# VectorE's side work regrouped by slot in the second mixers, with whole parameter rows in DRAM

## The reference, cut to what matters

```python
def _mamba(x, Win, convw, convb, Wx, Wdt, bdt, Alog, Dp, Wout):
    xz = x @ Win
    xi, z = jnp.split(xz, 2, axis=-1)
    xi = jax.nn.silu(_causal_dwconv(xi, convw, convb))
    xdbc = xi @ Wx
    dt_in = xdbc[..., :DT_RANK]
    Bm = xdbc[..., DT_RANK:DT_RANK + D_STATE]
    Cm = xdbc[..., DT_RANK + D_STATE:]
    dt = jax.nn.softplus(dt_in @ Wdt + bdt)
    A = -jnp.exp(Alog)
    y = _selective_scan(xi, dt, A, Bm, Cm, Dp)
    return y * jax.nn.silu(z) @ Wout
...
    yf = _mamba(x, fw_Win, fw_convw, fw_convb, fw_Wx, fw_Wdt, fw_bdt, fw_Alog, fw_D, fw_Wout)
    yf = _layernorm(yf + x, fwn_w, fwn_b)
    yb = _mamba(jnp.flip(x, 1), bw_Win, bw_convw, bw_convb, bw_Wx, bw_Wdt, bw_bdt, bw_Alog, bw_D, bw_Wout)
    yb = _layernorm(jnp.flip(yb, 1) + x, fwn_w, fwn_b)
    y = yf + yb
```

## Time and profile before

| | us |
|---|---|
| median of 3 runs | 3485.58 |
| lowest, highest | 3485.55, 3494.75 |
| the profiled execution | 3482.14 |
| its span in the profile | 3480.3 |

### The profile page before, as it was taken

The page is one execution under the profiler, slowest core; times in us unless marked ns, Lnnn a source line. Parts: engine busy times, 40 slices in busy tenths (PEclk is TensorE's granted clock), DMA queues, the critical chain, the costliest instruction groups (busy, mean ns, idle before and its releaser), DMA issues. The chain is left out here.

```text
span 3480.3 us, 25090 instructions
## 1 busy us (share of the span) xinstructions
PE 2788.0 (80%) x7782; PEld 1181.9 (34%) x7782; DVE 2847.1 (82%) x2257; ACT 1775.0 (51%) x2375; POOL 2241.3 (64%) x1102
## 2 busy tenths in 40 slices
PE   6677777666577888888888888788888787779899
PEld 2223222454223333333333333333333332234344
DVE  6999899542369999999999999999999999578300
ACT  5775776231355655555655555565555654233211
POOL 3696499001339889899889889788888898401000
PEclk7899799878879999999999999999999999889899
DMA  2011011247436656666756666665666666421000
GB/s 64 31 48 36 26 49 48 71 153 273 159 86 176 172 171 163 178 180 165 182 171 174 175 176 179 168 174 168 176 168 175 178 165 200 114 92 49 12 18 24
DMA packets 245973, 451.46 MB, mean 130 GB/s; under 512 B 22448, under 2 KB 51312, under 8 KB 245808
## 3 DMA queue, kind: packets, MB, share of 16 engines
q1 hardware_dynamic: 240080, 428.89, 43.8%
q0 software_dynamic: 5760, 20.97, 1.5%
HBM read 414.94 MB, written 34.87 MB: 129 GB/s over the span
## 5 line engine op out<-in xcount | busy, mean ns | idle before, releaser
L1394 POOL TENSOR_TENSOR mix_prod<-mix_spread,mix_h 128x1024 f32<-128x1024 f32 x512 | 1335.7, 2612 | 249.3 <-DVE mix_h L1818 118.7
L1926 PE MATMUL mix_banks<-mix_prod,kept_ident 128*128 128x512 f32 x2048 | 1035.9, 631 | 117.4 <-POOL mix_prod L1394 84.6
L1444 ACT ACTIVATE mix_side_in<-mix_dt,mix_neg_a 128x1024 f32<-128x1024 f32 x384 | 437.6, 1141 | 308.5 <-DVE mix_h L1818 305.1
L1926 PEld LDWEIGHTS mix_banks<-mix_prod,kept_ident 128*128 128x128 f32 x2048 | 396.6, 199 | 555.6 <-issue 296.5
L1804 DVE TENSOR_TENSOR mix_banks<-mix_banks,mix_dtu 128x1024 f32<-128x1024 f32 x384 | 466.6, 1215 | 9.6 <-PE mix_banks L1916 6.5
L1818 DVE TENSOR_TENSOR_SCAN mix_h<-mix_side_in,mix_state,mix_banks 128x1024 f32<-128x1024 f32 x192 | 450.6, 2347 | 17.4
L1818 DVE TENSOR_TENSOR_SCAN mix_h<-mix_side_in,mix_banks 128x1024 f32<-128x1024 f32 x192 | 439.0, 2286 | 19.2 <-ACT mix_side_in L1444 1.8
L410 POOL TENSOR_TENSOR mix_drive<-mix_drive,mix_du 128x1024 f32<-128x1024 f32 x128 | 304.8, 2399 | 150.7 <-ACT mix_drive L481 150.7
L1404 POOL TENSOR_TENSOR mix_side_in<-mix_spread,mix_dtu 128x512 f32<-128x512 f32 x256 | 340.5, 1330 | 13.4 <-issue 6.7
L1916 PE MATMUL mix_banks<-mix_parts,kept_sel 96*128 96x512 bf16 x384 | 153.9, 401 | 210.8 <-DVE mix_h L1818 203.3
L633 DVE TENSOR_TENSOR_SCAN mix_h<-mix_banks,mix_state,mix_drive 128x1024 f32<-128x1024 f32 x128 | 296.1, 2340 | 14.2 <-POOL mix_drive L410 9.3
(11 more groups left out here) (270 smaller groups left out, 4471.3 us busy)
## 6 DMA issues: line engine op xcount, KB each, us to landing
mix_spread<-par_rows SPq DMA_DIRECT2D x640, 512.0 KB, 5.9
mix_c_row<-c_rows SPq DMA_DIRECT2D x40, 512.0 KB, 3.5
exa_f<-f SPq DMA_DIRECT2D x32, 512.0 KB, 6.9
slot_outputs<-exa_inter POOLq DMA_DIRECT2D x32, 512.0 KB, 7.2
ln_zp<-slot_outputs SPq DMA_DIRECT2D x8, 2048.0 KB, 7.7
first_acc<-xT SPq DMA_DIRECT2D x8, 512.0 KB, 8.2
x_scratch<-first_acc POOLq DMA_DIRECT2D x8, 512.0 KB, 3.2
fw_scratch<-mix_res SPq DMA_DIRECT2D x8, 512.0 KB, 9.1
```

Source lines behind the costliest of these rows:

```text
L1394: pool.tensor_tensor(prod[:, un % 2, :], spread[:, i % SLOTS, :], h[:, un % HR, :], ALU.mult).then_inc(prod_ready, 1)
L1444: act.activation(drive[un % 2] if pooled(un) else side_in[:, un % 2, :], dt[:, at // NS, :], ACT.Exp, scale=neg_a[:, way(p), at:at + 1]).t ...
L1926: mm = pe.matmul(y_bank[:, hf, :], k.ident[:], half(prod[:, un % 2, :], hf), start=False, stop=True, skip_group_check=True)
```

## The change

Four things are changed, all in `mixer1`.
- Tables of VectorE's side work: `soft` of group 1 from slots (5, 6, 8) to (5, 8, 9), of group 2 from (15, 16, 19) to (16, 17, 20), of group 3 from (24, 25, 26) to (24, 25, 28). `conv` from (29, 30, 31), (35, 36, 37), (41, 42, 43) to (29, 32, 33), (36, 37, 38), (40, 41, 44). For the pass behind: `joined` of the first half from 32, 33 to 36, 37; of the second half `near_root` 29 to 30, `root_of` 41 to 40, `normed` 46, 47 to 48, 49, `joined` 48, 49 to 52, 53. `less_mid` from 55 to 56, and ScalarE's `split_low` behind it from 56 to 57. One pair of matmuls on TensorE goes from slot 37 to 38 and ScalarE's copy of it from 38 to 39.
- `par_rows` in DRAM holds one row of 1024 steps for each state, where it held two of 512. A load of a row takes one piece of 4 KB for a partition, and was two of 2 KB.
- The store of these rows is four DMAs of 16 partitions and was one of 64; SP makes it in slot 55 and not 53, and waits for it in slot 62.
- SP's other steps come later: `load_yf` in slots 32 and 42 (26 and 37), `store` in 41 and 57 (36 and 53).

```diff
-    par_rows = nc.dram_tensor("par_rows", (NP, 2, 2, NS, TT), F32, kind="Internal").ap()
+    par_rows = nc.dram_tensor("par_rows", (NP, 2, NS, TC), F32, kind="Internal").ap()
...
-                    if s == 26:
+                    if s == 32:
                         load_yf(p - 1, 0)
-                    if s == 36:
+                    if s == 41:
                         store(p - 1, 0)
...
-                if p + 1 < NP and s == 53:
+                if p + 1 < NP and s == 55:
                     sp.wait_ge(c_kept, p + 2)
-                    sp.dma_start(par_rows[p + 1].rearrange("k h n t -> (k h n) t"), rows[0:64, :]).then_inc(c_stored, 16)
-                    sp.wait_ge(c_stored, 16 * (p + 2))
+                    for kind in range(2):
+                        for hf in range(2):
+                            r0 = 32 * kind + NS * hf
+                            sp.dma_start(half(par_rows[p + 1, kind], hf), rows[r0:r0 + NS, :]).then_inc(c_stored, 16)
+                if p + 1 < NP and s == 62:
+                    sp.wait_ge(c_stored, 4 * 16 * (p + 2))
...
-                row = par_rows[un // UNITS, 1 if kind == "c" else 0, :, n:n + 1, :].rearrange("h o t -> o h t")
-                sp.dma_start(spread[:, i % SLOTS, :].rearrange("p (h t) -> p h t", h=2), row.broadcast_to((P, 2, TT))
+                row = par_rows[un // UNITS, 1 if kind == "c" else 0, n:n + 1, :]
+                sp.dma_start(spread[:, i % SLOTS, :], row.broadcast_to((P, TC))
...
-                    for hf, at in enumerate(((17, 20, 21, 22, 32, 33), (29, 41, 46, 47, 48, 49))):
+                    for hf, at in enumerate(((17, 20, 21, 22, 36, 37), (30, 40, 48, 49, 52, 53))):
...
-                    for g, at in ((1, (5, 6, 8)), (2, (15, 16, 19)), (3, (24, 25, 26))):
+                    for g, at in ((1, (5, 8, 9)), (2, (16, 17, 20)), (3, (24, 25, 28))):
```

More of the change, by code:

```diff
@@ L1145, in __init__ @@
             if p + 1 < passes:
-                for n, s in enumerate((25, 27, 32, 33, 34, 36, 37, 39)):
+                for n, s in enumerate((25, 27, 32, 33, 34, 36, 38, 39)):
                     order.append((s, 0, ("xi", p + 1, n // 2, n % 2)))
@@ L1320, in side @@
                 if p >= 1:
[L1321 removed]
+                    if s == 32:
                         load_yf(p - 1, 0)
[L1323 removed]
+                    if s == 41:
                         store(p - 1, 0)
[L1325 removed]
+                    if s == 42:
                         load_yf(p - 1, 1)
[L1327 removed]
+                    if s == 57:
                         store(p - 1, 1)
[L1329 removed]
+                if p + 1 < NP and s == 55:
                     sp.wait_ge(c_kept, p + 2)
[L1331 to L1332 removed]
+                    for kind in range(2):
[4 more added lines that the diff above has]
+                    sp.wait_ge(c_stored, 4 * 16 * (p + 2))
                 if p == WAY - 1 and s == 4:
@@ L1519, in keep_par @@
                 if p:
-                    act.wait_ge(c_stored, 16 * p)
+                    act.wait_ge(c_stored, 4 * 16 * p)
                 act.activation(rows[:], bank[0:96, :], ACT.Copy).then_inc(c_kept, 1)
@@ L1612, in side @@
                         tap_matrices(1)
-                    for n, s0 in enumerate((26, 28, 33, 34, 35, 37, 38, 40)):
+                    for n, s0 in enumerate((26, 28, 33, 34, 35, 37, 39, 40)):
                         if s == s0:
@@ L1772, in side @@
                 if ahead:
-                    for g, at in enumerate(((29, 30, 31), (35, 36, 37), (41, 42, 43))):
+                    for g, at in enumerate(((29, 32, 33), (36, 37, 38), (40, 41, 44))):
                         if s in at:
@@ L1777, in side @@
                         rest_of(p + 1)
-                    if s == 55:
+                    if s == 56:
                         less_mid(p + 1)
@@ L1947, in side @@
                 if ahead:
-                    for n, s0 in enumerate((25, 27, 32, 33, 34, 36, 37, 39)):
+                    for n, s0 in enumerate((25, 27, 32, 33, 34, 36, 38, 39)):
                         if s == s0:
```

2 lines of the change are left out of this document (removed).

## The result

| | before | after |
|---|---|---|
| median of 7 runs each, us | 3489.73 | 3500.55 |
| lowest to highest | 3485.55 to 3494.75 | 3499.22 to 3505.08 |
| the profiled execution (its span) | 3482.14 (3480.3) | 3505.08 (3503.3) |

The ratio is 1.0032, with a 95% interval of 1.0021 to 1.0044: slower by 10.8 us (7 to 15). The time is inside the range, near its upper end. The likeliest case was no change, which the prediction bounded at 0.3%; the measured 0.32% lies on that bound, and its interval reaches to both sides of it.

The account below looks back on a forecast made before the run. VectorE was taken to bound the second mixers, with about 71 us of port waiting (instruction time over its minimum, from taking turns with GpSimd) movable. Terms summed to +0.7 us, giving a forecast median of 3486 us, range 3460 to 3503.

Parts of the forecast that it names:

- (a): SP's later store of parameter rows: waits in slot 55 and nearly all left in 57 and 58 go, -12.8 us.
- (b): SP's later load of the forward result: GpSimd no longer starves, taps of slots 29 and 30 stop waiting, -5.0 us.
- (c): Whole rows in DRAM land in 4 to 5 us, not 5.9; VectorE waits less in slots 4 to 9, -8 us (0 to -15).
- (d): Moved joins (L1745): most of their 4.3 us of waiting goes, -3 us (0 to -4.3).
- (e): Slot 20: `soft` step behind `root_of` waits 2.2 us in each of 7 passes, +15.4 us (0 to 16.8).
- (f): Slots 36 and 37: a tap behind `joined` waits in passes 5 and 6, +8.8 us (0 to 9.6).
- (g): Pair of `root_of` and tap moved from slot 41 to 40 waits a whole product, +2.4 us (-11 to +4).
- (h): `soft` steps moved from slots 15, 16 to 16, 17 wait 19.8 us against 18.9, +0.9 us (-10 to +9).
- (i): The other moved side steps, some 40, start first in their slots at 0.05 us each, +2 us.
- random arrivals: Rival, chance 0.01: 11 moved steps meet GpSimd at random moments in each of 8 passes, waiting 88 us; 3574 us.
- GpSimd late in slots of kind 0 and 1: Rival, chance 0.19: side steps moved where GpSimd has product and half drive wait more; slots 8, 9, 16, 17 priced; 3502 us.
- The pairs cost nothing: Rival, chance 0.15: TensorE's add delays GpSimd's product over 0.6 us in slots 20, 36, 37, 40; both instructions pass; 3448 us.

## Why the prediction was right and wrong

The sum said +0.7 us, and 10.8 was measured; beside it, the port waiting grew by 20.6 to 25.3 us, for which VectorE's idle time gave back up to 8.4. By its steps, with the port waiting of the two profiled executions:

| step | predicted | seen |
|---|---|---|
| (a) store of rows | -12.8 | -10.0 here; -14.6 alone |
| (b) load_yf | -5.0 | -5.1, but slots 28, 32 and 33 +9.0 |
| (c) whole rows | -8 | -9.1 in slots 5 to 9; alone -4.9 there and -37 in all |
| (d) joins | -3 | -0.3 |
| (e) slot 20 | +15.4 | +24.6 |
| (f) slots 36, 37 | +8.8 | +9.1 |
| (g) slots 40, 41, 44 | +2.4 | +1.0 |
| (h) slots 15 to 17 | +0.9 | +4.1 |
| (i) others | +2 | +2 (what is left of +25.3) |

**Right** was the reading that port waiting is what can move most, and the price of the second two-SBUF instruction. L1710 takes 3.36 us in slot 20 in six of seven passes with a pass behind (predicted 3.4), L1707 3.01 in slot 17 (3.0), the tap behind `joined` 3.37 in slots 36 and 37; the rows land in 4.0 us (4 to 5) and GpSimd waits 2.8 us for them (under 10). Of the 17 pairs in slots 20, 36, 37 and 40, 14 pay; three don't (slot 20 of pass 6, slot 40 of passes 5 and 6), and the two of slot 40 are why (g) stayed under its +2.4. Term (a) held as a single edit within 2 us in its sum, but by luck in its parts: its 5.3 us of slots 57 and 58 belong to (c), as the run with the store later alone shows. The Trainium skill, in "SBUF — State Buffer", section "SBUF: two separate sides", has the port pair as an exclusive lock that its holder keeps for the whole instruction. The trace agrees: the second step waits 2.16 us, nearly the whole 2.35 of a product.

**Wrong** was (e), in "`root_of` starts at the scan's end" with the product 0.3 us behind it. I took this lateness from rows 4 and 5, slots 39 and 40, and put it on slot 20, where the changed tables leave slot 19 empty and slot 17 crowded. `root_of` waits 1.42 us in the mean there. The run with `near_root` in slot 19 showed where that comes from: the 1.8 us of step (h) in slot 17, with the 0.6 of `near_root` itself, stretch TensorE's idle time from 2.06 to 4.45 us, its first add runs at a lower granted clock, and GpSimd gets its buffers late. I had priced the wait of slot 17 and not who stands behind it. "I am wrong if those that stand first wait a microsecond" came true here, though not through random arrivals: it is the same place in all seven passes. The sign "within 5 us of 1951" failed as well, with VectorE busy for 1977.6 us.

**Wrong** was (b) in what it left out: the waits of slots 29 and 30 went, and new ones came in slots 32 and 33, which the sum had among the cheap moves of (i). In slot 32 of pass 1 the tap starts at 1376.08 and takes 3.32 us, because GpSimd began a product at 1375.97, 2.0 us after the scan that it needs. TensorE shows what kept it back: a projection (L1869) that waited 3.01 us for `near_root`, now in slot 30 and formerly in 29, ran at 2.75 us for four matmuls (1.88 elsewhere), and the add behind it ended at 1375.80.

```profile
1370.40 2.75 PE L1869 MATMUL mix_banks<-kept_xn,mix_win 128*128 128x512 f32 x4 [3.01 <-DVE mix_logv L1723]
1372.95 2.85 PE L1931 MATMUL mix_banks<-mix_prod,kept_ident 128*128 128x512 f32 x4
```

The move of `near_root` is not enough by itself. The run with the taps near their old slots leaves it in slot 30, and TensorE has the same 3.01 us of idle time there and the same slow matmuls (2.61 and 2.99 us), but GpSimd's product is in time, since the tap in slot 30 holds VectorE back. So it takes both: a projection that waits for `near_root`, and slots 30 and 31 emptied of taps, in which VectorE runs ahead. With `near_root` back in slot 29 and the taps as changed nothing was run, so the first half of this is read from the timeline and not shown by a run.

**Wrong in size** was (c), and by most. As the prediction has it, the rows' lateness costs in slots 4 to 9; the run with whole rows alone gained 37 us, with 15 us of port waiting in slots 15, 16, 29, 30, 57 and 58 and 5 to 13 us of VectorE's idle time besides. The upper end of 15 was too near because it was read from the three slots of the earlier trace rows alone. Against the second profile of before, whose time is 3.5 us over the median, port waiting (21.1) and idle time (13.1) make 34 of the 37; why idle time fell stays open. The miss was hidden by its counterpart. Rows, store and SP's other steps together are worth 50 us, the tables cost 59 on top of them, and the prediction had -25.8 ((a) to (c)) and +26.5 ((d) to (i)). The net came out right within 10 us by luck: both were too small by about as much.

Step (d) gave nothing: `joined` waits as much in slots 36, 37 and 52 as it had in 32, 33 and 48.

Of the rivals, none is what happened. "GpSimd late in slots of kind 0 and 1" comes nearest in time (3502), and its place in slots 16 and 17 partly held (23.0 us of waiting, between my 19.8 and its 28.2), but slots 8 and 9 did not keep their 15.3 (6.1). GpSimd was late in a slot of kind 0 where this rival had not priced it, in slot 20, and through TensorE's add, not through its own half drive. "The pairs cost nothing" and "random arrivals" fell: most pairs pay 2.1 to 2.2 us, and steps alone in their slot behind a timely GpSimd pay 0.3 or less.
